# Memory attention, its norms and top-1 router logits in one block, batch by batch; result rows scattered into the output; a loop start with two roots

## What is computed

```python
# hyperbolic attention (16 heads of 8)
diff_sq = maximum(q_norm_sq + k_norm_sq - 2.0 * qk, 0.0)
denom = maximum((1.0 - q_norm_sq) * (1.0 - k_norm_sq), 1e-06)
cosh_arg = maximum(1.0 + 2.0 * diff_sq / denom, 1.0)
attn = softmax(-arccosh(cosh_arg), axis=-1)
x = x + (attn @ v) @ Wo.T
# memory attention: C is a context of 32 slots per batch, X = layernorm(x)
sim = sigmoid(beta + alpha * einsum('bkd,btd->bkt', C, X))
mask = one_hot(argmax(sim, axis=1), 32, axis=1)
agg = einsum('bkt,btd->bkd', sim * mask, X) + C
out_k = agg / (sum(mask, axis=-1, keepdims=True) + 1.0)
x = x + X + einsum('bkt,bkd->btd', sim, out_k)
# top-1 mixture of 8 experts, xf = layernorm(x) as 2048 rows
e = argmax(xf @ Wg + bg, axis=-1)
x = x + gelu(xf @ W1[e]) @ W2[e]        # hidden size 512
```

## Time and profile before

| | |
|---|---|
| median of 3 runs | 1285.22 us (1282.93 to 1285.47) |
| profiled execution, own time | 1284.13 us |
| its span in the trace | 1281.7 us |
| busy PE / PEld | 947.0 us (74%) / 464.4 us (36%) |
| busy DVE | 973.9 us (76%) |
| busy ACT | 765.2 us (60%) |
| busy POOL | 571.5 us (45%) |
| mean granted TensorE clock | 0.717 of full speed |

### The profile page before, as it was taken

How to read it: one execution, slowest core, us unless ns; L and a number is a source line. 1 busy time by engine, 2 the same in 40 slices (tenths; PEclk the granted TensorE clock), 3 DMA queues, 4 the chain that set the end, 5 groups by cost and what they waited for, 6 DMA issues and landing times. The chain is left out here.

```text
span 1281.7 us, 16656 instructions
## 1 busy us (share of the span) xinstructions
PE 947.0 (74%) x5186; PEld 464.4 (36%) x5186; DVE 973.9 (76%) x2104; ACT 765.2 (60%) x995; POOL 571.5 (45%) x490
## 2 busy tenths in 40 slices
PE   5886955799997449992766788877888887445294
PEld 2553342455554339991300011111111111034294
DVE  5676678688883557775799999999899999756532
ACT  3303666266665314441625999999999999821041
POOL 0004100022221037651456888888888878200174
PEclk9997986599999559996855555566555556565598
DMA  6000001231100137762251000010000000020164
GB/s 189 15 1 1 0 1 42 67 87 57 45 26 2 58 122 237 237 200 84 82 161 49 25 24 25 29 43 26 25 25 25 25 25 1 1 68 27 54 175 133
DMA packets 61015, 80.70 MB, mean 63 GB/s; under 512 B 15049, under 2 KB 38012, under 8 KB 60672
## 3 DMA queue, kind: packets, MB, share of 16 engines
q1 hardware_dynamic: 51936, 67.85, 17.6%
q0 software_dynamic: 3968, 8.13, 2.0%
q10 hardware_dynamic: 5024, 3.67, 0.9%
HBM read 64.09 MB, written 15.34 MB: 62 GB/s over the span
## 5 line engine op out<-in xcount | busy, mean ns | idle before, releaser
L2813 POOL TENSOR_TENSOR hb_t<-hb_t,hb_r 128x512 f32<-128x512 f32 x248 | 362.3, 1501 | 69.2 <-ACT hb_r L2623 67.7
L2826 DVE TENSOR_SCALAR hb_dpos<-hb_psR 128x1024 f32<-128x1024 f32 x128 | 155.6, 1216 | 23.1 <-PE hb_psR L2548 18.4
L2572 PE MATMUL hb_psO<-hb_t,ha_va 128*9 128x512 f32 x512 | 113.6, 987 | 59.3 <-ACT hb_t L2652 55.1
L2557 PE MATMUL hb_psR<-ha_q,ha_k 20*128 20x512 bf16 x256 | 127.1, 596 | 40.8 <-DVE hb_dpos L2826 40.8
L2834 DVE SCALAR_TENSOR_TENSOR hb_t<-hb_psR,hb_dpos 128x1024 f32<-128x1024 f32 x128 | 154.9, 1210 | 0.0
L2149 ACT ACTIVATE ga_att<-ga_psB 128x512 f32<-128x512 f32 (+3 forms) x256 | 100.8, 453 | 67.7 <-PE ga_psB L2075 47.8
L2548 PE MATMUL hb_psR<-ha_q,ha_k 78*128 78x512 bf16 x256 | 128.0, 603 | 7.8 <-DMA ha_k<-hsx 3.5
L2170 DVE TENSOR_REDUCE ga_nm<-ga_psA 128x1 f32<-128x128 f32 (+3 forms) x256 | 113.0, 484 | 21.8 <-PE ga_psA L2053 20.4
L2652 ACT ACTIVATE hb_t<-hb_t 128x4096 f32<-128x4096 f32 (+2 forms) x32 | 111.2, 3522 | 0.0
L2843 DVE SCALAR_TENSOR_TENSOR hb_r<-hb_t 128x1024 f32<-128x1024 f32 x64 | 106.0, 1656 | 0.0
L2020 POOL TENSOR_SCALAR_AFFINE_SELECT ga_att<-ga_att 128x512 f32<-128x512 f32 x48 | 30.6, 637 | 133.8 <-ACT ga_att L2149 133.8
(11 more groups left out here) (477 smaller groups left out, 2088.9 us busy)
## 6 DMA issues: line engine op xcount, KB each, us to landing
m2x_e_w<-in_L_ffn_W_dram SPq DMA_DIRECT2D x78, 256.0 KB
m1x_e_w<-in_L_ffn_W_dram SPq DMA_DIRECT2D x23, 256.0 KB
ga_q<-qx SPq DMA_DIRECT2D x48, 96.0 KB
ha_q<-hqx SPq DMA_DIRECT2D x48, 96.0 KB
ha_k<-hkx SPq DMA_DIRECT2D x48, 96.0 KB
hy_fwd<-in_const_fwd_dram SPq DMA_DIRECT2D x1, 2048.0 KB
f_down<-in_L_ffn_W_dram ACTq DMA_DIRECT2D x4, 512.0 KB, 4.4
hsx<-hp_aparts SPq DMA_DIRECT2D x6, 288.0 KB
```

Of the source, the lines that this page charges most:

```text
L2557: mm = pe.matmul(psR[:, side_slot(n), i, :], k[SIDE:SIDE + SROWS, it % 2, i0 + i, P * c:P * c + P], q[SIDE:SIDE + SROWS, it % 2, i0 + i, : ...
L2572: mm = pe.matmul(psO[32 * i:32 * i + VW, :], va[:, CH * (it // G) + c, HPG * (it % G) + i, :], t[:, (2 * it + form) % T_QUADS, 2 * half + ...
L2813: half_sum = pool.tensor_tensor(tt, tt, rr, ALU.add)
L2826: dve.tensor_scalar(dpos[:, n % 2, :], psR[:, dist_slot(n), :, :].rearrange("p i t -> p (i t)"), 0.0, None, ALU.max).then_inc(dpos_ready, 1)
```

## The change

Three places change.

1. **Loop start.** In steps 0, 1 and 2 the quads of form 0 are treated as form 1: no product on DVE, two roots on ACT (`by_product` is true from step PLAIN = 3). `two_roots` waits for the last unit of its quad and, from the fourth quad on, for the sums of the quad three before. ACT's order at the start is roots (0,0), (0,1), (1,0), the table, logs and weights of step 0, roots (1,1), and then the loop from step 2. `inverses(1)` stands ahead of clip n = 2.
2. **Memory block.** Both norms, the memory attention and the router's logits, maximum and index stand in one block, batch by batch, with an order for each engine that is written out. ACT normalises (scale and shift per row, the deviation as exp of -0.5 ln), POOL forms the shifts and adds xn to x, turning of sim is a product with the identity, the counts of the gather share its PSUM bank, and xT holds two batches. SP loads the router's five tables there, ahead of the second weights, and stores for each batch xn and x side by side into `m1x_tokens`, whose rows are now 2D wide (1 KB). The router block of `mixture` begins at the cast of the choice. The full-width buffers xnT and chosen go.
3. **Results.** The gather brings xn and x of a token; DVE's copy of a result becomes an add of that x; POOL scatters it into the output itself, with padding rows sent beyond the last row and dropped (`bounds_check`). `m1x_outputs`, the fetch, the adds and the output's store go. XR is 8, and a gather into a used buffer waits for the result of the tile in it; the scatter of tile t stands behind the gather of tile t + 8. One more DVE operation in the router block (`line`) forms the targets.

The first mixture (top 2), which shares `mixture`, keeps its instructions.

```diff
-        self.tokens = nc.dram_tensor(name + "_tokens", [TOKENS, D], F32).ap()
+        self.direct = top == 1
+        self.RW = 2 * D if self.direct else D
+        self.tokens = nc.dram_tensor(name + "_tokens", [TOKENS, self.RW], F32).ap()
...
+                    if direct:
+                        sp.wait_ge(ex.kept, 32 * BATCH)
+                        return
...
+                    if direct:
+                        ch.tick(dve.scalar_tensor_tensor(out=line[:, :], in0=tile_of, scalar=float(P), in1=later[:, :], op0=ALU.mult, op1=ALU.add))
...
-            XR, WR, YR, DR = 6, 4, 4, 3
+            XR, WR, YR, DR = 8 if direct else 6, 4, 4, 3
...
+                        if t >= XR and direct:
+                            pool.wait_ge(y_ready, t - XR + 1)
+                        elif t >= XR:
                             pool.wait_ge(x_turned, t - XR + 1)
...
+                        if direct:
+                            pool.indirect_dma_start(out=out.rearrange("b t d -> (b t) d"), out_offset=where, in_=yo[:, t % YR, :], in_offset=None,
+                                                    bounds_check=TOKENS - 1, oob_is_err=False).then_inc(stored[t % YR], 16)
...
                         if t + XR < NT:
                             load(t + XR)
-                        if t >= 3:
+                        if direct:
+                            store(t)
+                        elif t >= 3:
                             store(t - 3)
...
-                            dve.tensor_copy(yo[:, t % YR, :], psY[:, t % 2, 0:D]).then_inc(y_ready, 1)
+                            dve.tensor_tensor(yo[:, t % YR, :], psY[:, t % 2, 0:D], xt[:, t % XR, D:RW], ALU.add).then_inc(y_ready, 1)
...
+            PLAIN = 3
+
+            def by_product(it, form):
+
+                return form == 0 and it >= PLAIN
...
+                    def two_roots(it, form):
+                        act.wait_ge(t_ready, max(n for n in range(UNITS * it, UNITS * it + UNITS) if place(n)[1] == form) + 1)
+                        if 2 * it + form >= R_QUADS:
+                            act.wait_ge(sum_ready, 2 * QUAD * (2 * it + form - R_QUADS + 1))
...
                     prepare()
-                    for it in range(STEPS + 3):
+                    roots(0, 0)
+                    roots(0, 1)
+                    roots(1, 0)
+                    act.preload_act_table_set("natural_log_exp_and_others")
+                    logs(0, 0)
+                    logs(0, 1)
+                    weights(0, 0)
+                    weights(0, 1)
+                    roots(1, 1)
+                    for it in range(2, STEPS + 3):
...
-                        if n == 4:
+                        if n == 2:
                             inverses(1)
...
-                        if 2 <= n <= TOTAL + 1 and place(n - 2)[1] == 0:
+                        if 2 <= n <= TOTAL + 1 and by_product(*place(n - 2)[0:2]):
                             product(n - 2)
...
+                ex.fetch_router(sp)
+                ex.fetch_weights(sp)
+                where = ex.tokens.rearrange("(p g) d -> p g d", p=P)
+                for b in range(BATCH):
+                    sp.wait_ge(norm_ready[1], CH * b + CH)
+                    sp.wait_ge(x_ready, b + 1)
+                    sp.dma_start(where[:, quad(b), 0:D], xn[:, quad(b), :]).then_inc(ex.kept, 16)
+                    sp.dma_start(where[:, quad(b), D:2 * D], x[:, quad(b), :]).then_inc(ex.kept, 16)
...
                 for b in range(BATCH):
+                    turn(0, b)
+                    scores(b)
+                turn_sim(0)
+                gather(0)
+                turn_sim(1)
+                gather(1)
+                read_out(0)
+                turn_sim(2)
+                gather(2)
+                read_out(1)
+                pe.wait_ge(ex.params, ex.PARAMS)
+                turn(1, 0)
+                route(0)
+                turn_sim(3)
+                gather(3)
+                read_out(2)
+                turn(1, 1)
+                route(1)
+                read_out(3)
+                for b in range(2, BATCH):
+                    turn(1, b)
+                    route(b)
...
+                    act.activation(logv[:, n, quad(b)], mv[:, n, quad(b), 1], ACT.Ln, bias=eps[:, 0:1]).then_inc(log_ready[n], 1)
+                    act.wait_ge(log_ready[n], b + 1)
+                    act.activation(rstd[:, n, quad(b)], logv[:, n, quad(b)], ACT.Exp, scale=-0.5).then_inc(rstd_ready[n], 1)
...
+                    for g in range(CH * b, CH * b + CH):
+                        act.activation(xn[:, g, :], x[:, g, :], ACT.Identity, scale=rstd[:, n, g:g + 1], bias=shift[:, n, g:g + 1]).then_inc(norm_ready[n], 1)
...
+                    pool.wait_ge(norm_ready[0], CH * b + CH)
+                    pool.tensor_tensor(x[:, quad(b), :], x[:, quad(b), :], xn[:, quad(b), :], ALU.add).then_inc(x_kept, 1)
...
+                moments(0, 3)
+                choose(0)
+                choose(1)
+                update(0)
+                choose(2)
+                add_read(0)
+                moments(1, 0)
+                update(1)
+                choose(3)
+                add_read(1)
+                moments(1, 1)
+                update(2)
+                dve.wait_ge(ex.params, ex.PARAMS)
+                expert(0)
+                add_read(2)
+                moments(1, 2)
+                update(3)
+                expert(1)
+                add_read(3)
+                moments(1, 3)
+                expert(2)
+                expert(3)
```

More of the change, by code:

```diff
@@ L1351, in mixture @@
             growth = s.sb("growth", [P, TILES])
+            line = s.sb("line", [P, NT])
             ps = s.ps("ps", [P, 512])
@@ L1566, in _ @@
                             sp.dma_start(w[:, t % WR, n, :], ex.weights[n][bass.ds(e, 1), :, :].rearrange("a d f -> d (a f)")).then_inc(w_loaded[t % WR], 16)
[L1567 to L1572, removed]
+                    if not direct:
+                        fetch(sp, 0)
                 @block.gpsimd
@@ new lines, in turn_sim, with gather @@
+                def turn_sim(b):
+                    pe.wait_ge(sim_ready, b + 1)
+                    for c in range(CH):
+                        mm = pe.matmul(psS[rows(b), P * c:P * c + P], sim[:, CH * b + c, :], ident[:, :], start=True, stop=True)
+                    mm.then_inc(sim_turned, 1)
+                def gather(b):
+                    pe.wait_ge(hot_ready, 2 * b + 2)
+                    for c in range(CH):
+                        pe.matmul(psA[rows(b), 0:D], e[:, CH * b + c, :], xn[:, CH * b + c, :], start=(c == 0), stop=(c == CH - 1))
+                    for c in range(CH):
+                        mm = pe.matmul(psA[rows(b), D:D + 1], hot[:, CH * b + c, :], ones[:, :], start=(c == 0), stop=(c == CH - 1))
+                    mm.then_inc(gathered, 1)
@@ L3057, in _ @@
-                mm.then_inc(gathered, 1)
-                pe.wait_ge(simT_ready, 1)
-                pe.wait_ge(row_ready, 1)
-                for b in range(BATCH):
-                    rows = slice(CTX * b, CTX * b + CTX)
-                    for c in range(CH):
-                        mm = pe.matmul(psO[:, b, D * c:D * c + D], simT[rows, c, :], row_out[rows, :], start=True, stop=True)
-                    mm.then_inc(read, 1)
+                for b in range(BATCH):
+                    turn(0, b)
+                    scores(b)
@@ new lines, in expert @@
+                def expert(b):
+                    q = quad(b)
+                    dve.wait_ge(routed, b + 1)
+                    dve.tensor_tensor(ex.lg[:, q, :], psZ[:, b % 2, P:P + CH * EXPERTS].rearrange("p (g e) -> p g e", g=CH), over(ex.rb[:, :], CH), ALU.add).then_inc(lg_ready, 1)
+                    dve.wait_ge(lg_ready, b + 1)
+                    for g in range(CH * b, CH * b + CH):
+                        ch.tick(dve.max(ex.mx[:, g, :], ex.lg[:, g, :]))
+                    ch.join()
+                    for g in range(CH * b, CH * b + CH):
+                        ch.tick(dve.max_index(ex.ix[:, g, :], ex.mx[:, g, :], ex.lg[:, g, :]))
```

371 lines of the change are left out of this document (249 added, 122 removed).

## The result

The changed kernel took 1268.68 us (median of 4 runs, 1267.75 to 1269.25) against 1285.35 for the kernel before on the same chip: a ratio of 0.9874, 95% interval 0.9858 to 0.9889. The forecast was 1260.9, its range 1252 to 1271. The direction and the range held; of the 24 us that were forecast between the medians, 17 came.

What follows compares the result with a forecast made beforehand. It took ACT to bound the loop, engines taking turns the memory stage and POOL the expert stage. 4.6 + 11.8 - 0.1 - 2.6 - 0.4 + 9.9 = 23.2 off 1284.1 gave 1260.9 us, range 1252 to 1271.

Steps and rivals of the forecast that it cites:

- Part 1: Start of the hyperbolic loop: ACT enters its gapless part earlier, a gain of 4.6 us (2 to 6).
- the walk: Step-by-step engine timelines: ACT's roots at 656.1, 666.3, 681.1 in the loop; PE's transposes and scores to 1148.5 in the memory block.
- Part 2: Memory block and router logits: batchwise merging ends the block 52.5 us after its start, a gain of 11.8 us.
- the higher clock for part of the second half: Memory block: PE partly at 2.4 GHz, so the block ends at 1180.8, between 1183.5 (lower clock) and 1178 (higher).
- What was costed at nothing: Memory block: POOL's adds of x and xn, 6 us in all, and the stores of tokens stay hidden.
- Part 3: Expert stage: losses of 2.6 us for fewer early gathers and 0.4 for wider gathered rows.
- 2 x 1.3: Expert stage: 38 instead of 36 indirect DMAs stand behind the first result, a loss of 2.6 us.
- Part 4: Tail: fetch, adds and output store go; landing 2.24 and close 0.6 remain, a gain of 9.9 us (9.1 to 10.5).
- the block's close, which lies between 0 and 1.4; I take 0.6: Tail: time to close the last block, 0.6 us, beside the last scatter's landing of 2.24.
- rival (b): Memory block of 56 to 58 us, scatters 0.2 dearer, or loop start gaining only 2: 1264 to 1272 us; chance 0.22.
- (c): Expert stage: POOL's gathers and scatters take twice as long, so the kernel is slower, 1303 us at +0.98 each; chance 0.03.
- (d): Merged parts gain nothing: loop start 0, memory block 62, tail 9; 1281 to 1284 us; chance 0.02.

Runs made afterwards that it cites:

- all together: The changed kernel with the last block closed without POOL's DRAIN, 11 buffers for gathered rows and a reordered memory block; 1259.13 us, ratio 0.9806 to the kernel before.
- the experiment on the last load: The changed kernel with ACT's load of the ln and exp table put back ahead of the last step's logs; 1268.59 us, ratio 0.9865 to the kernel before.
- The other order: The changed kernel with the same memory-block instructions reordered on PE, DVE and ACT; 1266.11 us, ratio 0.984 to the kernel before.
- the kernel of narrow rows: The changed kernel gathering 512 B rows of xn alone, without DVE's add of x and the four stores of x; 1267.03 us, ratio 0.985 to the kernel before.

## Why the prediction was right or wrong

The range held; the point was 7.8 us under the median. In the order of the steps:

- **Ahead of the loop: +1.8, not forecast and not the change's.** Nothing differs there. In the twelve profiled executions, all with the same code there, the first ratio starts anywhere from 642.9 (11 buffers) to 646.0 (all together). A sum made against one execution carries that scatter.
- **Part 1, loop's start: right, with 0.9 more that it did not name.** Relative to the first ratio, ACT's three entries came within 0.1 us of the walk (656.1, 666.3 and 681.1, with the shift of 1.8 added), and the load for the roots of step 3 stands 98.3 behind the ratio instead of 103.2: 4.9, against 4.6. The remaining 0.9 came at the loop's very end. It is not the dropped load; behind DVE's last reciprocal the wait of its last copy of the output for PE's products is 2.72 us instead of 3.56. The 24 products themselves, shown with the experiment on the last load, are 0.80 shorter, at a higher clock.
- **Part 2, memory block: direction right, a term mis-sized.** PE's first half kept to the walk: it turned sim for the first time 19.2 us behind the first statistics, where 20.2 were forecast. The term that was mis-sized is the price of "turning sim and reading out 8 passes x 1.99/13 = 1.2 each". That row is a window of 4 us with 13 passes in it, too few and too short to carry a price. At 0.50 (1.2 GHz) the turning takes 1.92 and the read-out 2.04, at 1.00 1.06 and 1.15; a gather takes 2.2 at 0.50 (1160.54 to 1162.76), not 1.7. From start to start, and for the router's products by their row, a batch is then 2 x 1.1 (transposes) + 1.84 (scores) + 1.71 (turning sim) + 2.22 (gather) + 1.98 (read-out) + 1.87 (router) = 11.8 us of PE at the lower level, and PE's work in the block is 47, not 40.5. The clock paid a part of it back: it rose in a stretch in which PE was busy 3.50 of 3.50 us and stood at 1.00 (2.4 GHz) for the 6 us from 1147, and again about 1164. The choice of "the higher clock for part of the second half" was thus right and the work under it too small. The block ended 54.6 us after its start instead of 52.5; the barrier took 1.9 instead of 1.5. (The prediction's own sum for the lower clock comes to 1183.0, not 1183.5, which changes little: it chose a point between that and 1178.) The same order of the block gave 56.6 to 56.7 us up to the cast in five executions and 57.9 in two, in which the clock rose 25 us behind the first statistics instead of 21.8. The other order shows that at least 1.9 of the block lay in who waits for whom. How much the wrong price is worth beside that is not shown, as the halved read-out decided nothing.
- **What was costed at nothing: right.** POOL's four adds were over at 1141.0, ten us ahead of the first add of a read-out, at 1.27 us each. The Trainium skill, GPSIMD Engine Reference, section 3.1, has an add 1.96 times slower on GPSIMD; this is 2.2 times DVE's 0.57, and between the page's estimate and the 1.48 of the earlier trace rows. The store of tokens was hidden: the sort took 16.63, against 16.54 before.
- **Part 3, expert stage: right in kind, 1.2 short.** 38 indirect DMAs stood behind the first result, at 1.314 instead of 1.299 each, so 3.2 in place of 2.6. The 0.6 between these is as much as two pauses of POOL near the end, 0.71 and 0.47 us at 1254.73 and 1256.18 where 0.30 is usual. There the chain of waits runs from a gather's landing (4.16 from 1247.80) over PE to DVE's result at 1257.03, so the last scatters went by results and not by POOL. The first result came 1.0 later, where 0.4 was taken: the third gather landed 0.8 later than before (4.76 for 3.94), and in the kernel of narrow rows the first result came 1.9 sooner. The Trainium skill, DMA: Bandwidth & Descriptors, section Anatomy of one DMA, would make 64 KB more 0.15 us (an estimate); the runs show 0.65 to 0.9 beside the loads of the weights, and the measurement decides. What the prediction priced as "2 x 1.3" is in the trace an idle time of 4.03 us on POOL, and 11 buffers take it back.
- **Part 4, tail: the largest error.** The step that failed is "the block's close, which lies between 0 and 1.4; I take 0.6", for which it names no row. The rows landed as forecast (2.1 us), but the close is POOL's DRAIN of 3.81 us. Without the DRAIN the close is 0.5 (2.6 less the landing), so the 0.6 fits all of it but the DRAIN. The DRAIN was in the trace of before, at 1271.6, in a view of queues that counts no busy time, and it had cover: the fetch, the adds and the store. The prediction took the cover away without looking for what it covered. None of its rivals had this mechanism; the time fell among those of rival (b), for a reason that (b) did not name.

Rivals (c) and (d) did not come true: a gather's issue stayed at 0.97, a scatter's with the bounds check at 1.01.

## What to carry to other kernels

When a change removes the last stage of a kernel, list what every queue still does behind the point that becomes the last, with the queues' own rows and not the busy ones: a close that was hidden is late next. An engine that issues one after the other needs as many requests in hand as fit into the time to the first result; here 11 buffers instead of 8 were worth 4.0 us. Price PE's passes by rows of the same shape at a known level of the clock, not by a short window's busy time over its count.

## What the runs showed of the hardware

POOL's DRAIN at a block's end took 3.81 us behind 46 indirect DMAs, 6.43 behind 78 and 3.16 where another DRAIN had left 38: 0.083 us for each since the one before. Its work can run beside the landing of the rows: given to do so it ended 3.8 behind the end of the last issue, and the kernel's end came 1.4 us earlier. A DRAIN behind eight gathers, though, ended 2.1 us behind the last issue and not 0.7, so the price per DMA isn't the whole of it. And in the one execution with half of each read-out taken from PE the granted clock did not rise a second time in the block, as it did in seven with the whole: the router's products of batch 1 took 1.87 us instead of 1.06.
